# Causal mask of an attention's second pass: from mask matmuls to GpSimd selects, and the second pass first in each slot

## The chip, the cores and the metric

The kernel runs on one core of one Trainium2 chip. The metric is the device time of one execution in microseconds; the kernel before has a median of 624.34 us over three executions (624.0 to 624.88).

## The reference, cut to what matters

Two transformer layers on x of 4 sequences of 512 tokens with 128 channels (a state-space mixer and a mixture of experts, then attention and a second mixture of experts), each part behind an adaptive layer norm. The change touches the attention of the second layer alone: 16 heads of 8 channels, rotary positions, causal softmax.

```python
q = apply_rope(q); k = apply_rope(k)
scores = jnp.einsum('bhqd,bhkd->bhqk', q, k) / jnp.sqrt(dk)
causal = jnp.tril(jnp.ones((S, S), dtype=bool))
scores = jnp.where(causal, scores, -jnp.inf)
probs = jax.nn.softmax(scores, axis=-1)
attn = jnp.einsum('bhqk,bhkd->bhqd', probs, v)
return attn.transpose(0, 2, 1, 3).reshape(B, S, D) @ W_o.T
```

## The kernel before, in words

The five engines and SyncE each have their own program and meet at semaphores. What lies before attention and behind it is untouched by the change.

Attention works on 16 steps s = 4b + g: sequence b, group g of four heads. It has two passes. The **first pass** finds the maximum of each query's scores: `scores` (L1619) computes 16 score tiles of a step in 10 units on TensorE, each unit into one bank of a ring of three PSUM banks; VectorE's `maximum` (L1151) adds a mask that lies in SBUF and reduces each tile. Four small VectorE ops (`max_parts`, L1165 to L1172) split the negated maxima into three bf16 parts, `maxima_T` (L1629) transposes them, ScalarE evacuates them (L730), and SyncE writes them with four DMAs (L340) as three more rows of the augmented queries, the m rows. The keys have three rows of ones there (`k_ones`), so that a product of 51 rows gives the score less its maximum.

The **second pass** computes the transposed scores. `scores_T` (L1650) takes one key tile and one pair of heads, into two of the four PSUM banks 4 to 7; ahead of them four matmuls (L1645: two 64-column halves for each of two heads) write a causal mask of 0 and -1e30 into the 128 columns of the diagonal tile, and the scores are accumulated on top. ScalarE takes the exponential (`probs`, L701) of both heads into one of four buffers of pt. `weighted_values` (L1664) multiplies a pair of these by the values.

All engines follow one order, of rounds `it` from -2 to 16 and 8 slots i each: the first pass is of step it + 2, the second of step it. In slot i TensorE does the unit or units of `scores`, then `scores_T(8*it + i)`, which waits for the exponential of two slots before and, in slot 0, for the m rows, then in odd slots the weighted values of a pair of slots (in slot i those of i - 3 and i - 2), and the transposes and projections that have a place in this slot: `maxima_T` in 2, `o_T` (L1673) in 3, the projections of sequences 2 and 3 in rounds 2 and 6. ScalarE evacuates the finished output (L724) in slot 1, and VectorE divides it by its denominators in slot 3 (L1181, L1185), when `o_T` is there. In rounds 5, 9 and 13 VectorE also prepares the router's input (`router_input`, L367, L372, L386, L1123, L1128) in slots 2 to 6: in slot 4, L386 waits for GpSimd's `ln_rstd` (L379, L381).

GpSimd has little to do there: `rotate`, `rest` and `last_part` (L475, L481, L486) for the rotated queries and keys of each sequence, and `ln_rstd`, each as soon as its input is there. SyncE writes the parts of queries and keys to DRAM (12 DMAs, L312) and reads them back in the attention's layout (8 DMAs, L325); for sequences 2 and 3 it does so between the m rows of steps 4 and 5, and of 8 and 9.

Of the kernel before, what the change touches and what calls it, by code (L numbers as in the profile page):

```python
# [9 lines left out]
ALU = mybir.AluOpType  # L10
# [3 lines left out]
P = 128  # L14
B, S, D = 4, 512, 128
# [40 lines left out]
BPACK = [("identb", 128), ("causal", 256), ("half", 64), ("sel0", 1024)]  # L56
# [10 lines left out]
def adaln_kernel(nc, x_in, mod_in, mixw_in, moe0_in, attn_in, moe1_in, const_in, bconst_in, kones_in, out):  # L67
    with ExitStack() as ctx:
# [219 lines left out]
        def _(sp):  # L288
# [13 lines left out]
            for k in range(2):  # L302
                for hh in range(2):
                    sp.dma_start(kaug[HALF * hh + KR:HALF * hh + KM, k, :, :], kones_in).then_inc(sem("k_ones"), 16)
# [94 lines left out]
        def _(pool):  # L399
# [69 lines left out]

            def rotate(i):  # L470
# [27 lines left out]
            for b in range(1, B):  # L498
                if b == 3:
                    ln_rstd(pool, 4, 0)  # L500
                for stage in (rotate, rest, last_part):
                    stage(2 * b)
                    stage(2 * b + 1)
            for b in range(1, B):
                ln_rstd(pool, 4, b)
# [792 lines left out]
        def _(pe):  # L1298
# [308 lines left out]
            def scores(s, i):  # L1607
                b, g = divmod(s, QG)
                if g == 0 and i == 0:
                    pe.wait_ge(sem(f"aug_first{b % 2}"), 16 * 4 * (b // 2 + 1))  # L1610
                    pe.wait_ge(sem("k_ones"), 64)
# [21 lines left out]
            def scores_T(u):  # L1633
# [8 lines left out]
                for qh in range(2):  # L1642
                    for hh in range(2):
                        bank, lo = 4 + 2 * (u % 2) + hh, HALF * hh
                        pe.matmul(ps[:, bank, HALF * qh:HALF * (qh + 1)],  # L1645
                                  w["causal"][lo:lo + HALF, qh * P:(qh + 1) * P], w["half"][lo:lo + HALF, :],
                                  start=(qh == 0), stop=True, skip_group_check=True)
                for hh in range(2):
                    bank, lo = 4 + 2 * (u % 2) + hh, HALF * hh
                    mm = pe.matmul(ps[:, bank, 0:n], kaug[lo:lo + KM, b % 2, 2 * g + jp, kt * P:(kt + 1) * P],  # L1650
                                   qaug[lo:lo + KM, b % 2, 2 * g + jp, kt * P:S], start=False, stop=True,
                                   skip_group_check=True)
                mm.then_inc(sem("st_ps"), 1)

            def weighted_values(m):
# [5 lines left out]
                pe.wait_ge(sem("probs"), 2 * (m + 1))  # L1661
# [34 lines left out]
            for it in range(-2, 17):  # L1696
# [3 lines left out]
                for i in range(8):  # L1700
                    if it + 2 < 16:
                        for u in at_slot[i]:
                            scores(it + 2, u)
                    if 0 <= it < 16:
                        scores_T(8 * it + i)
# [59 lines left out]
def shape_constants():  # L1765
# [21 lines left out]
    for e in range(8):  # L1787
        for piece in range(3):
# [3 lines left out]
        "causal": np.concatenate([np.where(k[None, :] > k[:, None] % HALF + HALF * qh, NEG, 0.0) for qh in range(2)],  # L1792
                                 axis=1),
# [70 lines left out]
```

## Time and profile before

| | us |
|---|---|
| median of three executions | 624.34 |
| profiled execution | 620.97 |
| its span, first to last instruction | 619.2 |
| TensorE matmul, busy | 479.0 |
| VectorE, busy | 410.3 |
| ScalarE, busy | 278.0 |
| GpSimd, busy | 197.7 |
| mask matmuls (L1645), 512 of them, busy | 48.6 |
| attention, slot (0,0) to the last weighted values | 323.8 to 509.1 |

The busy times are from the page's first part. Matmuls overlap in the array and their ends are modelled, so that the times of TensorE's groups can't be added up; starts are better read than durations. The profiled execution lies 3.4 us below the median.

### The profile page before, as it was taken

The numbers are of one execution on the slowest core, as the hardware profiler recorded it, in microseconds if no ns is written. First come the engines' busy times: TensorE is split into PE (matmuls) and PEld (weight loads), VectorE is DVE, ScalarE is ACT, GpSimd is POOL, SyncE is SP. The second block draws the span as 40 slices with busy tenths as digits, with TensorE's granted clock in tenths as the row PEclk, the third lists the DMA queues.
The fourth block names the chain that finished last, engine by engine and source line by source line (L and its number), as shares of the span: only waits on it lengthen the run. The fifth ranks groups of instructions, "written<-read, shape, count | busy, mean of one in ns | idle before, by whom it ended". The sixth has DMA issues, their size and how long they took to land.

```text
span 619.2 us, 10103 instructions
## 1 busy us (share of the span) xinstructions
PE 479.0 (77%) x3167; PEld 283.4 (46%) x3167; DVE 410.3 (66%) x1363; ACT 278.0 (45%) x510; POOL 197.7 (32%) x254
## 2 busy tenths in 40 slices
PE   4697779886989999995589994998599786009990
PEld 4554567765634444442334442344245235009990
DVE  4788668996456767677787893788488804305543
ACT  2477876642235454532225681476357471002330
POOL 4300059995105544445500120031000000453443
PEclk9888899996599999999756996599779898558996
DMA  9500000001500000002860035006200000022014
GB/s 361 142 1 1 0 2 2 2 0 35 244 1 0 1 2 0 0 1 70 210 130 2 3 105 103 2 4 173 34 3 3 2 2 1 31 86 76 32 36 148
DMA packets 25083, 31.75 MB, mean 51 GB/s; under 512 B 2444, under 2 KB 22860, under 8 KB 24508
## 3 DMA queue, kind: packets, MB, share of 16 engines
q1 hardware_dynamic: 23784, 28.52, 16.4%
q0 software_dynamic: 1248, 2.59, 1.3%
q8 instruction: 27, 0.44, 0.3%
q14 instruction: 24, 0.20, 0.1%
HBM read 19.42 MB, written 11.48 MB: 50 GB/s over the span
## 4 chain that ended last, share of the span: by engine, by line
PE 52%; DVE 18%; issue 8%; ACT 7%; DMA 5%; POOL 5%; SPq 5%; DVEq 0%; ACTq 0%; POOLq 0%
PE ps L1664 5%; PE ps L1547 5%; PE ps L1551 4%; PE ps L1535 4%; DVE moe L1151 3%; PE ps L1748 3%; PE ps L1619 3%; PE ps L1570 3%; DVE rows L386 2%; POOL slots_x L512 2%; PE ps L1759 2%; PE ps L1650 2%; SPq L312 2%; PE ps L1352 2%; DMA arena<-arena 2%
## 5 line engine op out<-in xcount | busy, mean ns | idle before, releaser
L1151 DVE CUSTOM_DVE_ANT_0 moe<-ps,const 128x512 bf16<-128x512 f32 (+3 forms) x256 | 113.0, 487 | 25.9 <-PE ps L1619 24.8
L701 ACT ACTIVATE arena<-ps 128x256 f32<-128x256 f32 (+3 forms) x128 | 86.4, 702 | 66.6 <-PE ps L1650 65.7
L1619 PE MATMUL ps<-arena 48*128 48x128 bf16 (+3 forms) x256 | 61.1, 346 | 15.3 <-DVE arena L1151 13.9
L1645 PE MATMUL ps<-bconst 64*128 64x64 bf16 x512 | 48.6, 203 | 17.3 <-DMA arena<-arena 15.6
L461 POOL TENSOR_TENSOR arena<-arena 128x512 f32<-128x512 f32 x30 | 38.1, 1270 | 68.4 <-DVE arena L1053 68.2
L1650 PE MATMUL ps<-arena 51*128 51x128 bf16 (+3 forms) x256 | 57.0, 328 | 0.0
L1664 PE MATMUL ps<-arena 128*32 128x512 f32 (+3 forms) x512 | 55.2, 507 | 0.9 <-ACT arena L701 0.6
L379 POOL TENSOR_SCALAR rs<-mv 128x4 f32<-128x4 f32 x20 | 5.3, 264 | 139.7 <-DVE mv L372 139.2
L1619 PEld LDWEIGHTS ps<-arena 48*128 48x128 bf16 x256 | 17.2, 98 | 68.5 <-DVE arena L1151 42.8
L1645 PEld LDWEIGHTS ps<-bconst 64*128 64x128 bf16 x512 | 31.6, 102 | 32.1 <-DMA arena<-arena 17.5
L1044 DVE SCALAR_TENSOR_TENSOR arena<-ps,arena 128x512 f32<-128x512 f32 x32 | 22.1, 692 | 27.7 <-ACT arena L677 27.7
L749 ACT ACTIVATE arena<-ps 128x512 f32<-128x512 f32 x23 | 13.7, 597 | 54.6 <-PE ps L1748 35.2
L672 ACT ACTIVATE arena<-ps,moe 128x512 f32<-128x512 f32 x32 | 22.0, 687 | 34.5 <-PE ps L1547 34.5
L861 DVE SCALAR_TENSOR_TENSOR arena<-ps,mixw,arena 128x511 f32<-128x511 f32 (+2 forms) x48 | 33.2, 745 | 5.0 <-ACT arena L569 5.0
L1547 PE MATMUL ps<-arena,moe 128*128 128x512 f32 x64 | 32.9, 595 | 1.0 <-DVE arena L1038 1.0
L475 POOL TENSOR_TENSOR moe<-moe 128x512 f32<-128x512 f32 x8 | 10.2, 1270 | 72.4 <-DVE moe L1070 72.4
L1551 PE MATMUL ps<-arena,moe 128*128 128x512 f32 x64 | 32.7, 591 | 0.0
L1535 PE MATMUL ps<-arena,moe 128*128 128x512 f32 x64 | 32.5, 592 | 0.0
L518 POOL DMA_INDIRECT tokens_y<-arena,token_at x23 | 22.0, 957 | 32.1 <-DVE arena L1286 30.8
L1739 PE MATMUL ps<-const,arena 128*128 128x128 f32 x23 | 6.5, 293 | 29.3 <-DMA arena<-slots_x 29.3
L677 ACT ACTIVATE arena<-ps,moe 128x512 f32<-128x512 f32 x32 | 22.0, 687 | 13.0 <-PE ps L1551 13.0
L1748 PE MATMUL ps<-arena 128*128 128x128 f32 x184 | 26.1, 288 | 0.5 <-DVE arena L1282 0.3
(242 smaller groups left out, 1111.2 us busy)
## 6 DMA issues: line engine op xcount, KB each, us to landing
qk_parts<-arena SPq DMA_DIRECT2D x48, 128.0 KB, 2.3
arena<-qk_parts SPq DMA_DIRECT2D x16, 288.0 KB, 6.1
arena<-moe_in SPq DMA_DIRECT2D x1, 4100.0 KB, 14.0
moe<-moe_in SPq DMA_DIRECT2D x1, 1936.0 KB, 14.1
arena<-qk_parts SPq DMA_DIRECT2D x16, 96.0 KB, 2.2
slots_x<-zeros SPq DMA_DIRECT2D x1, 1518.0 KB, 20.5
arena<-slots_x SPq DMA_DIRECT2D x3, 396.0 KB, 4.3
const<-const_in SPq DMA_DIRECT2D x1, 1067.0 KB, 8.6
```

What stands on the lines that cost most here:

```text
L461: pool.tensor_tensor(yacc[:, ts], yacc[:, ts], pr[:, i % 2, :], ALU.add).then_inc(sem("yacc"), 1)
L701: act.activation(pt[:, u % 4, :, 0:n], ps[:, 4 + 2 * k:6 + 2 * k, 0:n], ACT.Exp, scale=ATT_SCALE).then_inc(sem("probs"), 1)
L861: v.scalar_tensor_tensor(out=acc[b % 2][:, c, s:S], in0=ps[:, c, 0:S - s], scalar=w["conv_w"][:, 4 * c + 3 - s:4 * c + 4 - s], in1=acc[b % ...
L1151: v.tensor_tensor_reduce(out=junk[:, done % 2, 0:n], in0=ps[:, k, col:col + n], in1=w["mask"][:, (3 - qt) * P:4 * P], scale=1.0, scalar=3 ...
L1535: pe.matmul(ps[:, 6 + i % 2, :], w["w2"][:, e * D:(e + 1) * D], gT[:, i % 2, :], start=True, stop=True).then_inc(sem("p2_ps"), 1)
L1547: pe.matmul(ps[:, 2 + i % 2, :], w["w1"][:, e * D:(e + 1) * D], xm[:, i % 2, :], start=True, stop=True).then_inc(sem("p1_ps"), 1)
L1551: pe.matmul(ps[:, 4 + i % 2, :], w["w3"][:, e * D:(e + 1) * D], xm[:, i % 2, :], start=True, stop=True).then_inc(sem("p3_ps"), 1)
L1619: mm = pe.matmul(ps[:, k, col:col + n], qaug[lo:lo + KR, b % 2, 2 * g + j // 2, qt * P:(qt + 1) * P], kaug[lo:lo + KR, b % 2, 2 * g + j // ...
L1645: pe.matmul(ps[:, bank, HALF * qh:HALF * (qh + 1)], w["causal"][lo:lo + HALF, qh * P:(qh + 1) * P], w["half"][lo:lo + HALF, :], start=(qh ...
L1650: mm = pe.matmul(ps[:, bank, 0:n], kaug[lo:lo + KM, b % 2, 2 * g + jp, kt * P:(kt + 1) * P], qaug[lo:lo + KM, b % 2, 2 * g + jp, kt * P:S] ...
L1664: mm = pe.matmul(ps[32 * j:32 * j + 32, 3, kt * P:S], va[:, b % 2, kt, 4 * (s % QG) + j, :], pt[:, (2 * m + j // 2) % 4, j % 2, 0:n], star ...
L1748: mm = pe.matmul(ps[:, j % 2, q * P:(q + 1) * P], w1[:, j % 2, q * P:(q + 1) * P], xT[:, j % 2, :], start=True, stop=True)
```

## The change

The four mask matmuls in front of `scores_T` are taken out, with their two constants; the scores no longer accumulate on a mask. In their place GpSimd runs one affine select on each slot's exponentials: in the 128 columns of the diagonal tile, for both heads, it keeps an element where the query is not before the key and writes 0 elsewhere. The weighted values wait for the selects (`masked`) and no more for the exponentials (`probs`). GpSimd's program becomes a loop over the same rounds and slots, in which `rotate`, `rest`, `last_part` and `ln_rstd` have fixed places behind the select of a slot. On TensorE `scores_T` moves ahead of `scores` in every slot. The semaphore `k_ones` is merged into `aug_first0`.

```diff
--- before.py
+++ after.py
@@ -53,7 +53,7 @@
     "const": [("ident", 128), ("tri", 128), ("after", 128), ("cos", 512), ("sin", 512), ("iota", 8),
               ("mask", 512), ("segment", NT * E1), ("full", NT), ("block", NBLK), ("number", NT), ("spare", NBLK)],
 }
-BPACK = [("identb", 128), ("causal", 256), ("half", 64), ("sel0", 1024)]
+BPACK = [("identb", 128), ("sel0", 1024)]
 
 
 def offsets(fields):
@@ -301,7 +301,8 @@
 
             for k in range(2):
                 for hh in range(2):
-                    sp.dma_start(kaug[HALF * hh + KR:HALF * hh + KM, k, :, :], kones_in).then_inc(sem("k_ones"), 16)
+                    sp.dma_start(kaug[HALF * hh + KR:HALF * hh + KM, k, :, :], kones_in)\
+                        .then_inc(sem("aug_first0"), 16)
 
             def parts_out(b, i):
 
@@ -467,6 +468,15 @@
                     pool.memset(va[:, :, :, :, DK:DK + 1], 1.0).then_inc(sem("va_clear"), 1)
 
 
+            nothing = pool.to_reg(0.0)
+
+            def causal(u):
+
+                pool.wait_ge(sem("probs"), u + 1)
+                own = pt[:, u % 4, :, 0:P]
+                pool.affine_select(own, own, pattern=[[0, 2], [1, P]], base=0, channel_multiplier=-1,
+                                   compare_op=ALU.is_ge, fill=nothing).then_inc(sem("masked"), 1)
+
             def rotate(i):
                 a = i % 2
                 pool.wait_ge(sem("rope"), 2 * (i + 1))
@@ -495,14 +505,26 @@
             last_part(1)
             ln_rstd(pool, 3, 2)
             ln_rstd(pool, 3, 3)
-            for b in range(1, B):
-                if b == 3:
-                    ln_rstd(pool, 4, 0)
-                for stage in (rotate, rest, last_part):
-                    stage(2 * b)
-                    stage(2 * b + 1)
-            for b in range(1, B):
-                ln_rstd(pool, 4, b)
+            for stage in (rotate, rest, last_part):
+                stage(2)
+                stage(3)
+            for it in range(17):
+                for i in range(8):
+                    if it < 16:
+                        causal(8 * it + i)
+                    if it in (2, 6):
+                        b = (it + 6) // 4
+                        if i in (3, 7):
+                            rotate(2 * b + i // 4)
+                    if it in (3, 7):
+                        b = (it + 5) // 4
+                        if i in (2, 3):
+                            rest(2 * b + i - 2)
+                        elif i in (5, 6):
+                            last_part(2 * b + i - 5)
+                    if it in (5, 9, 13) and i == 5:
+                        ln_rstd(pool, 4, it // 4 - 1)
+            ln_rstd(pool, 4, B - 1)
 
             pool.wait_ge(sem("posu"), 1)
             pool.wait_ge(sem("numbers"), 2)
@@ -1607,8 +1629,7 @@
             def scores(s, i):
                 b, g = divmod(s, QG)
                 if g == 0 and i == 0:
-                    pe.wait_ge(sem(f"aug_first{b % 2}"), 16 * 4 * (b // 2 + 1))
-                    pe.wait_ge(sem("k_ones"), 64)
+                    pe.wait_ge(sem(f"aug_first{b % 2}"), 64 * (b // 2 + 2 - b % 2))
                 elif g == 1 and i == 0:
                     pe.wait_ge(sem(f"aug{b % 2}"), 16 * 4 * (b // 2 + 1))
                 k = ring_bank("mx", s, i)
@@ -1639,17 +1660,10 @@
                     pe.wait_ge(sem(f"m_rows{s % 2}"), 64 * (s // 2 + 1))
                 if u >= 2:
                     pe.wait_ge(sem("probs"), u - 1)
-                for qh in range(2):
-                    for hh in range(2):
-                        bank, lo = 4 + 2 * (u % 2) + hh, HALF * hh
-                        pe.matmul(ps[:, bank, HALF * qh:HALF * (qh + 1)],
-                                  w["causal"][lo:lo + HALF, qh * P:(qh + 1) * P], w["half"][lo:lo + HALF, :],
-                                  start=(qh == 0), stop=True, skip_group_check=True)
                 for hh in range(2):
                     bank, lo = 4 + 2 * (u % 2) + hh, HALF * hh
                     mm = pe.matmul(ps[:, bank, 0:n], kaug[lo:lo + KM, b % 2, 2 * g + jp, kt * P:(kt + 1) * P],
-                                   qaug[lo:lo + KM, b % 2, 2 * g + jp, kt * P:S], start=False, stop=True,
-                                   skip_group_check=True)
+                                   qaug[lo:lo + KM, b % 2, 2 * g + jp, kt * P:S], start=True, stop=True)
                 mm.then_inc(sem("st_ps"), 1)
 
             def weighted_values(m):
@@ -1658,7 +1672,7 @@
                 n = S - kt * P
                 if i == 0 and s >= 1:
                     pe.wait_ge(sem("ot"), s)
-                pe.wait_ge(sem("probs"), 2 * (m + 1))
+                pe.wait_ge(sem("masked"), 2 * (m + 1))
                 pe.wait_ge(sem("va"), b + 1)
                 for j in range(4):
                     mm = pe.matmul(ps[32 * j:32 * j + 32, 3, kt * P:S], va[:, b % 2, kt, 4 * (s % QG) + j, :],
@@ -1698,11 +1712,11 @@
                     transposes(3, 2, bank=4)
                     transposes(3, 3, bank=4)
                 for i in range(8):
+                    if 0 <= it < 16:
+                        scores_T(8 * it + i)
                     if it + 2 < 16:
                         for u in at_slot[i]:
                             scores(it + 2, u)
-                    if 0 <= it < 16:
-                        scores_T(8 * it + i)
                     if i % 2 == 1 and 0 <= 4 * it + i // 2 - 1 < 64:
                         weighted_values(4 * it + i // 2 - 1)
                     if i == 2 and 0 <= it + 1 < 16:
@@ -1789,9 +1803,6 @@
             sel0[8 * piece + e, e, :] = 1.0
     bconst = {
         "identb": np.eye(P),
-        "causal": np.concatenate([np.where(k[None, :] > k[:, None] % HALF + HALF * qh, NEG, 0.0) for qh in range(2)],
-                                 axis=1),
-        "half": k[:, None] % HALF == np.arange(HALF)[None, :],
         "sel0": sel0.reshape(P, -1),
     }
     fc = np.concatenate([np.asarray(const[n], np.float32) for n, _ in PACKS["const"]], axis=1)
```

## Rows read from the trace of the kernel before

**Rows 1.** rounds 0, 1, 2, 11: length, busy PE PEld DVE ACT POOL, clock, DMA, GB/s

```profile
323.82:334.86 11.04, 10.05 (x94) 4.47 (x96) 8.27 (x41) 6.11 (x9) 0.00 (x0) 0.50 0.00 1
334.86:343.16 8.30, 8.05 (x107) 3.95 (x107) 7.30 (x34) 5.92 (x10) 0.00 (x0) 0.94 0.01 4
343.16:355.28 12.12, 12.12 (x116) 5.03 (x118) 10.52 (x43) 6.58 (x11) 1.99 (x2) 1.00 0.01 3
...
461.31:469.73 8.42, 7.80 (x108) 3.76 (x109) 7.85 (x39) 6.36 (x11) 0.00 (x0) 1.00 0.01 3
```

**Rows 2.** timeline of round 11: start us, us, engine line op form xcount [idle before]

```profile
461.79 0.66 ACT L701 ACTIVATE arena<-ps 128x256 f32<-128x256 f32 x2 [0.20 <-PE ps L1650]
...
462.61 0.17 DVE L1167 SCALAR_TENSOR_TENSOR arena<-arena 128x16 f32<-128x16 f32 x1
...
465.65 0.26 DVE L1181 RECIPROCAL arena<-ps 128x16 f32<-128x16 f32 x1 [0.34 <-PE ps L1673]
```

**Rows 3.** the page, granted clock in 40 slices of 15.5 us, in tenths

```profile
PEclk9888899996599999999756996599779898558996
```

**Rows 4.** chain of waits, 358 to 384 us: start us, us, what

```profile
358.45 0.58 ACT arena L730
...
368.50 0.60 SPq L312
...
377.53 5.54 DMA arena<-arena
...
383.12 0.29 PE ps L1645 x4
```

**Rows 5.** waits of TensorE in attention: us in total, times, longest

```profile
PE ps L1645 <- DMA arena<-arena: 15.6, 2, 8.3
```

**Rows 6.** timeline of TensorE, full clock at 355.6, half clock at 383.7

```profile
355.60 0.23 PE L1645 MATMUL ps<-bconst 64*128 64x64 bf16 x4
...
355.67 0.22 PE L1650 MATMUL ps<-arena 51*128 51x128 bf16 x2
...
383.74 0.31 PE L1645 MATMUL ps<-bconst 64*128 64x64 bf16 x2
...
383.87 0.29 PE L1650 MATMUL ps<-arena 51*128 51x128 bf16 x1
```

**Rows 7.** timeline of round 13, slots 4 to 7

```profile
485.34 1.51 ACT L701 ACTIVATE arena<-ps 128x768 f32<-128x768 f32 x2 [0.90 <-PE ps L1650]
...
485.88 0.23 POOL L379 TENSOR_SCALAR rs<-mv 128x4 f32<-128x4 f32 x1 [39.76 <-DVE mv L372]
...
487.26 1.12 DVE L386 TENSOR_SCALAR rows<-x,mv,rs 128x128 f32<-128x128 f32 x4 [0.81 <-POOL rs L381]
...
490.33 0.50 PE L1619 MATMUL ps<-arena 48*128 48x384 bf16 x1 [0.82 <-DVE arena L1151]
...
490.85 0.61 PE L1650 MATMUL ps<-arena 51*128 51x512 bf16 x1
```

**Rows 8.** GpSimd's groups by line and form: busy us, mean ns

```profile
L423 POOL TENSOR_TENSOR arena<-arena,mixw 128x256 f32<-128x256 f32 x16 | 11.7, 729 | 0.0
...
L459 POOL COPY arena<-arena 128x512 f32<-128x512 f32 x2 | 1.2, 608 | 3.0 <-DVE arena L1053 3.0
```

**Rows 9.** timeline of the end of attention

```profile
508.04 1.07 PE L1664 MATMUL ps<-arena 128*32 128x512 f32 x8 [0.60 <-ACT arena L701]
```

**Rows 10.** line L386 alone: duration ns min/median/max, first and last start

```profile
L386 DVE TENSOR_SCALAR rows<-x,mv,rs x48: 315/344/1189, 121.2 to 518.7; 128x128 f32<-128x128 f32 x48
```

**Rows 11.** timeline of VectorE beside GpSimd, at 303 and at 355 us

```profile
303.08 5.31 DVE L386 TENSOR_SCALAR rows<-x,mv,rs 128x128 f32<-128x128 f32 x6
...
303.58 2.26 POOL L481 TENSOR_TENSOR moe<-moe,arena 128x512 f32<-128x512 f32 x2
...
354.56 1.28 POOL L475 TENSOR_TENSOR moe<-moe 128x512 f32<-128x512 f32 x1 [4.53 <-DVE moe L1070]
...
355.10 0.56 DVE L1151 CUSTOM_DVE_ANT_0 moe<-ps,const 128x384 bf16<-128x384 f32 x1
```

## The prediction

> **What bounds the kernel now.** I read the page first: of 619.2 us, attention with its two interleaved passes is the stretch from slot (0,0) at 323.8 us to the last weighted values at 509.1 us, and all that the diff touches lies in it. (I write (it,i) for slot i of round it.) Then the windows, one for each round [rows 1]: at full clock a plain round takes 8.3 to 8.4 us, of which VectorE is busy 7.3 to 7.9; round 11 leaves it 8.42 - 7.85 = 0.57 us idle, 0.34 of it in front of the reciprocal, which waits for o_T [rows 2]. TensorE also looks full there (7.80), but its ends are modelled. In rounds 2 and 6, where it has the projections too, it is the later one (12.12 of 12.12). At half clock (round 0, 0.50) it is the bound as well: 10.05 of 11.04. The page's clock row [rows 3] and the windows put about 30 of the 128 slots at half clock.
>
> The chain of waits shows something that no engine's speed changes [rows 4]: from the evacuation of mT(4) in (3,2) at 358.45 SyncE issues 4 + 12 + 8 + 4 DMAs one behind the other, and (5,0) starts when the last has landed, at 383.12. TensorE waits 8.3 us there, and nearly as long again in (9,0): 15.6 us in two waits [rows 5]. What is won between (3,2) and (5,0) or (7,2) and (9,0), 28 slots in all, makes these waits longer and ends nothing earlier. 100 slots are left in which time can be won or lost.
>
> **The change part by part.** The sum is made against the profiled execution (620.97 us around a span of 619.2), which is 3.4 us below the median of 624.34; the difference is added to the median.
>
> *512 mask matmuls go.* A slot loses two 64-column matmuls in each row group, and the groups run side by side: from the first mask matmul to the scores behind it are 355.67 - 355.60 = 0.07 us at full clock, 383.87 - 383.74 = 0.13 at half [rows 6]. The page's 48.6 us of busy time for the line is pipeline depth counted over and over. Outside the two fixed stretches I count 23 half-clock slots with TensorE last (rounds 0, 5, 9, 10 and 13/14 in part): 3.0 us; and 27 at full clock (rounds 2, 6, 14, 15): 1.9. In the others VectorE is last and the edit is worth nothing. The half clock ends in the trace at moments of its own and not after so much work, so I take a quarter off the first: **-4.1 us**. Bounds: 0, and 23 x 0.13 + 77 x 0.07 = -8.4.
>
> *The second pass goes first in each slot.* ScalarE gets its scores before TensorE stands at a ring bank that VectorE still reads. Of VectorE's idle 0.57 us a plain round can give back half (bounds 0 and all): five rounds, -1.2. In rounds 5, 9 and 13 the scores of slot 7 wait at 490.33 and both second-pass matmuls (to 490.85) come behind them [rows 7]; now they are done before: 0.5 each, -1.5. Sum **-2.7**. Against it: in (5,0) and (9,0) the first-pass matmul used to be issued before the wait for the m rows and now stands behind it: 0.4 us of work at half clock each, **+0.8** (bounds 0 and 1.2).
>
> *128 selects on GpSimd.* The trace has none. From below, the one-input COPY of 128x512 at 608 ns makes about 0.36 us for 256 elements; from above, the two-input op on 512 elements, 1.27. The nearest row is the two-input op on 256 elements, 0.73 [rows 8]; with one input less I take 0.6, and 0.15 for two semaphores. 128 x 0.6 = 77 us lie beside other work: the pair that the weighted values need was exponentiated two slots before. It shows where ScalarE is last: behind the 1.02 us exponential of slot 7 in (it,1). In rounds with a first pass, the exponentials start some 0.3 us earlier by the new order and pay for it; in (15,1) I take 0.5, and behind the very last exponential all 0.75, since the weighted values at 508.04 already wait for it [rows 9]: **+1.25** (bounds 0.5 and 2.8). In the Trainium skill, GPSIMD Engine Reference, section 7 gives compare-and-select bodies 1.03 to 2.03 cycles an element; an estimate from that page is 0.2 to 0.45 us for 256, and the sum would be about 3 us lower; no run here shows it yet.
>
> *ln_rstd of rounds 5, 9, 13 moves behind a select.* GpSimd is strictly in order. Today it starts when the moments are there and VectorE's L386 in slot 4 waits for it until 487.26; variance and power take it from 485.88, 1.4 us [rows 7]. Now it stands behind causal(8it+5), that is behind the exponential of slot 5, which ends at 485.34 + 1.51 = 486.85, perhaps 0.25 earlier by the new order. 486.6 + 0.07 + 0.6 + 1.4 = 488.7: 1.4 us later. Behind L386 are queued the maxima of slots 5 to 7, which free the ring for TensorE. Three rounds: **+4.2** (bounds 0, if the delay is covered, and 6).
>
> *GpSimd is now busy beside VectorE.* L386 takes 344 ns in the median, and up to 1189 ns; the long ones lie in 303.08 to 308.39, 5.31 us for six of them under GpSimd's back-to-back ops of 1.1 to 1.3 us [rows 10, 11]. So some VectorE ops wait for a whole GpSimd op. The maxima (L1151) don't: 0.56 us under a GpSimd op like elsewhere [rows 11]. Exposed are the router's ops in rounds 5, 9, 13 (four L386, two products and sums, the residual sum) and the four small ops that split the maxima in slots 0 and 1 (L1165 to L1172). The exponentials of slots 7, 0 and 1 come close together (two in 1.0 us from 461.79, [rows 2]), so four selects stand back to back on GpSimd just where L1167 runs (462.61) and, before it, L1165; these ops never met GpSimd in the trace. Bounds for a round: 0 and 4 x 0.6 = 2.4; I take 0.7, two of them caught for a little over half a select. VectorE is last in some 7 rounds outside the fixed stretches: **+4.9**. The router's ops: 0.8 in each of three rounds (bounds 0 and 2), **+2.4**. In the Trainium skill, SBUF — State Buffer, section "Who interferes with whom" has this as an exclusive port pair: a VectorE op in a two-port mode or with two SBUF inputs against a GpSimd op that reads SBUF, while an op with one SBUF input goes free. The trace agrees: 1189 ns for L386, and no effect on L1151, which reads PSUM and one SBUF tile.
>
> *Rotate, rest, last_part between selects, k_ones on aug_first0, a narrower bconst.* In rounds 2/3 and 6/7 GpSimd gets 16 selects of 0.6 and the six old ops of some 1.2: 16.8 us of work in some 21: the last part is there about 1 us before SyncE issues its last DMA of the parts at 368.50 [rows 4]. Cover: SyncE's own issues. 0; if a select takes 0.9, 3 us late.
>
> Sum: -4.1 - 2.7 + 0.8 + 1.25 + 4.2 + 4.9 + 2.4 = **+6.75**; 624.34 + 6.75 = **631.1 us**.
>
> **The rivals.**
> - *TensorE's order paces every round* (for: 7.80 of 8.42 us busy in round 11; against: VectorE's 7.85 [rows 1]). All 100 slots pay: -8.4, the order -2.7, +0.8, +1.25, half of the ln_rstd term since VectorE has room, +2.1: -7.0, **617.3**. It decides if VectorE's small ops don't wait for GpSimd and a select stays below 0.4 us. Chance 0.13.
> - *A short select and no port waits on the small ops* (for: COPY at 608 ns; against: L386's 1189 ns). The terms of 4.9 and 2.4 go, 1.0 less for the shorter select: -1.5, **622.8**, up to 624.5 with a few waits. Chance 0.17, 0.10 of it within 0.2%.
> - *A long select, 0.9 us or more* (for: 0.73 to 0.81 us for 256 elements with two inputs). Port terms half as much again (+3.7), ln_rstd +0.9, tail +0.6, and the parts of rounds 3 and 7 late by 10 x 0.3 less the 1 us of room, twice (+4): **640**; from 1.04 us on GpSimd would pace every slot. Chance 0.14.
> - *The clock comes back one step later* after the waits in rounds 5 and 9, with less for TensorE to do: 6.8 us at 11.04 instead of 8.30 a round is 1.7 us, twice: **634.5**. Chance 0.09.
>
> **How the numbers follow.** My forecast has 0.47, between 627 and 635. Faster by over 0.2% (1.25 us, about what a measurement of this kernel can tell from no change): 0.13 + 0.07 = 0.20. Within it: 0.10 + 0.02 = 0.12. Slower: 0.68. The range takes in most of the first rival and the long select: 619.5 to 642.
>
> **What would show it.** The select's mean on GpSimd (0.6). Plain rounds at full clock: 8.4 us before, 8.8 to 9.2 after, with L1165, L1167, L1170 and L1172 above 0.2 us. L386 in rounds 5, 9, 13 starting about 1.4 us later behind the moments, and longer. The waits of some 8 us at (5,0) and (9,0) still there, each a little longer where the stretch before has become faster. The last weighted values 0.75 us behind the last exponential. I am wrong if the small ops keep their 0.18 us and plain rounds fall below 8.2.

## The result: 1% slower, by a sum whose terms were partly wrong

Changed kernel: 631.22 us in the median of 4 runs, against 624.61 us for the kernel before on the same chip, ratio 1.0132 (95% interval 1.0087 to 1.0176). Two later comparisons on other chips gave 1.0085 (1.005 to 1.0121) and 1.0103 (1.0064 to 1.0141). Weighted by their intervals the three make **1.0103 ± 0.0023**, that is 6.4 us of 623. The predicted ratio was 631.1 / 624.34 = 1.0108. Executions more than 1.5% longer than the fastest of their kernel are left out of the ratios; in the second comparison these were three of twelve, and with them its medians are 629.43 and 623.17 us, a ratio of 1.0100.

The edit moves the line numbers. In the changed kernel L477 is the select, L723 the exponential, L1173 the maximum of the first pass (L1151 before), L1640 the first pass's scores (L1619), L1665 the second pass's (L1650), L1650 `maxima_T` (L1629), L752 the evacuation of its result (L730), L1678 the weighted values (L1664), L380 and L382 the two operations of ln_rstd (L379, L381), L387 the router's normalisation (L386), and L1187, L1189, L1192 and L1194 the four small operations that split the maxima (L1165 to L1172).

The windows of the changed kernel answer to [rows 1] (columns as there: stretch and length, busy time of PE, PEld, DVE, ACT and POOL with the number of instructions, granted clock, DMA share, GB/s): rounds 0, 1, 2, 11, and then 13 and 15.

```profile
323.28:333.89 10.61, 9.44 (x61) 2.95 (x62) 8.26 (x40) 5.88 (x9) 3.26 (x8) 0.50 0.01 2
333.89:344.71 10.82, 10.46 (x76) 3.63 (x73) 7.53 (x33) 6.41 (x10) 2.91 (x8) 0.63 0.01 3
344.71:356.52 11.81, 11.78 (x84) 3.93 (x81) 10.54 (x43) 6.57 (x10) 4.42 (x9) 1.00 0.01 2
...
463.72:472.10 8.38, 7.26 (x76) 2.85 (x72) 7.87 (x39) 6.15 (x10) 3.20 (x9) 1.00 0.01 3
...
482.05:496.36 14.31, 8.70 (x75) 2.83 (x74) 12.20 (x51) 6.17 (x10) 4.82 (x10) 0.85 0.00 1
...
504.05:512.74 8.69, 6.58 (x60) 1.82 (x60) 0.55 (x2) 5.70 (x10) 3.61 (x9) 1.00 0.00 0
```

Round 0, at half clock under TensorE, fell from 11.04 to 10.61 us, and round 2 from 12.12 to 11.81. The plain round 11 did not grow to the 8.8 to 9.2 us that I had given as the mark of my theory: 8.42 became 8.38. Round 1 grew by 2.5 us because the full clock came back 6 us later in this execution (0.63 instead of 0.94); it came back as late in two of the three profiles of this kernel, and in one of a kernel beside it, so I take nothing from it. Round 13 went from 13.24 to 14.31, and round 15 to the end of attention from 8.29 to 8.69.

The select is shorter than I took, and VectorE waits longer for ln_rstd. First the page's group of the select, then the waits of VectorE in attention (engine, line, waited for: us in total, times, longest), which were 2.4 us in three before:

```profile
L477 POOL TENSOR_SCALAR_AFFINE_SELECT arena<-arena 128x256 f32<-128x256 f32 x128 | 51.9, 410 | 134.6 <-ACT arena L723 133.5
```

```profile
DVE rows L387 <- POOL rs L382: 5.9, 3, 2.2
```

The chain of waits in round 5 (start us, us, what) shows the path that I had priced: exponential of slot 5, select, variance and power of ln_rstd, then the four normalisations on VectorE, with the maxima behind them.

```profile
392.77 0.82 ACT arena L723
393.59 0.06 issue
393.65 0.41 POOL arena L477
394.06 0.21 POOL rs L380
394.27 0.07 issue
394.34 1.05 POOL rs L382
...
395.76 0.93 DVE rows L387 x3
396.69 0.33 DVE moe L1173
```

TensorE's waits for the DMAs in attention stand nearly as [rows 5] had them, 16.3 us in four against 15.6 in two; the one in front of (5,0) lasts 8.4. Its waits for the maxima of the first pass, which free the ring, were 7.9 us in 11 before, and are 12.3 in 10 now:

```profile
PE ps L1665 <- DMA arena<-arena: 16.3, 4, 8.4
PE ps L1640 <- DVE arena L1173: 12.3, 10, 3.3
PE ps L1650 <- DVE arena L1194: 7.4, 6, 1.7
PE ps L1678 <- POOL arena L477: 2.5, 4, 1.0
```

### The profile page after: what moved, and what is told of

Its sections match the earlier page's. It is cut to its first block, busy times and chain, and to the rows that moved or that the text cites. A ratio compares the mean times of both kernels' runs of the same rounds, so it can differ in the third digit from the quotient of the medians.

```text
span 624.8 us, 9208 instructions
## 1 busy us (share of the span) xinstructions
PE 473.6 (76%) x2655; PEld 268.4 (43%) x2655; DVE 415.2 (66%) x1363; ACT 277.3 (44%) x510; POOL 248.7 (40%) x382
## 4 chain that ended last, share of the span: by engine, by line
PE 52%; DVE 18%; issue 9%; ACT 6%; DMA 6%; POOL 5%; SPq 5%; DVEq 0%; POOLq 0%; ACTq 0%
PE ps L1678 5%; PE ps L1569 4%; PE ps L1573 4%; PE ps L1557 4%; DVE moe L1173 3%; PE ps L1762 3%; PE ps L1640 3%; PE ps L1773 2%; DVE rows L387 2%; PE ps L1665 2%; POOL slots_x L534 2%; PE ps L1592 2%; PE ps L1374 2%; SPq L313 2%; DMA arena<-arena 2%
## 5 line engine op out<-in xcount | busy, mean ns | idle before, releaser
L1173 DVE CUSTOM_DVE_ANT_0 moe<-ps,const 128x512 bf16<-128x512 f32 (+3 forms) x256 | 113.0, 486 | 25.3 <-PE ps L1640 24.9
L723 ACT ACTIVATE arena<-ps 128x256 f32<-128x256 f32 (+3 forms) x128 | 85.5, 700 | 63.4 <-PE ps L1665 62.6
L477 POOL TENSOR_SCALAR_AFFINE_SELECT arena<-arena 128x256 f32<-128x256 f32 x128 | 51.9, 410 | 134.6 <-ACT arena L723 133.5
L1640 PE MATMUL ps<-arena 48*128 48x128 bf16 (+3 forms) x256 | 59.3, 351 | 19.5 <-DVE arena L1173 18.3
L1665 PE MATMUL ps<-arena 51*128 51x128 bf16 (+3 forms) x256 | 44.6, 332 | 18.7 <-DMA arena<-arena 16.3
L1678 PE MATMUL ps<-arena 128*32 128x512 f32 (+3 forms) x512 | 56.3, 517 | 3.2 <-POOL arena L477 2.5
L1665 PEld LDWEIGHTS ps<-arena 51*128 51x128 bf16 x256 | 12.9, 97 | 70.1 <-ACT arena L723 25.7
L1640 PEld LDWEIGHTS ps<-arena 48*128 48x128 bf16 x256 | 21.7, 103 | 37.1 <-DVE arena L1173 30.5
L422 POOL TENSOR_TENSOR arena<-arena 128x256 f32<-128x256 f32 x16 | 12.4, 773 | 44.2 <-DVE arena L866 40.5
L1350 PE MATMUL ps<-const,rows 128*128 128x128 f32 x64 | 14.9, 393 | 13.9 <-DVE rows L387 10.4
```

What stands on the lines that cost most here:

```text
L477: pool.affine_select(own, own, pattern=[[0, 2], [1, P]], base=0, channel_multiplier=-1, compare_op=ALU.is_ge, fill=nothing).then_inc(sem(" ...
L723: act.activation(pt[:, u % 4, :, 0:n], ps[:, 4 + 2 * k:6 + 2 * k, 0:n], ACT.Exp, scale=ATT_SCALE).then_inc(sem("probs"), 1)
L1173: v.tensor_tensor_reduce(out=junk[:, done % 2, 0:n], in0=ps[:, k, col:col + n], in1=w["mask"][:, (3 - qt) * P:4 * P], scale=1.0, scalar=3 ...
L1640: mm = pe.matmul(ps[:, k, col:col + n], qaug[lo:lo + KR, b % 2, 2 * g + j // 2, qt * P:(qt + 1) * P], kaug[lo:lo + KR, b % 2, 2 * g + j // ...
L1678: mm = pe.matmul(ps[32 * j:32 * j + 32, 3, kt * P:S], va[:, b % 2, kt, 4 * (s % QG) + j, :], pt[:, (2 * m + j // 2) % 4, j % 2, 0:n], star ...
```

## The experiments

Each was timed beside the kernel before, and the ratios are against it.

### Which part costs: four kernels on one chip

**ln_rstd at slot 3 of its round instead of slot 5**

```diff
-                    if it in (5, 9, 13) and i == 5:
+                    if it in (5, 9, 13) and i == 3:
                         ln_rstd(pool, 4, it // 4 - 1)
```

> The changed kernel, with ln_rstd of rounds 5, 9 and 13 placed behind the select of slot 3 instead of slot 5. Theory (ln_rstd queued behind selects holds VectorE): the wait of L387 for it falls from 5.9 us in three times to about 3, and the kernel gains 2.5 to 3.5 us: 628. Rival (latency of the selects before the weighted values is what costs): no more than 1 us, 630 to 631. Rival (the clock): times scatter as before, with no link to this edit.

Measured: 1.0042 (1.0012 to 1.0072); VectorE's waits for it fell from 5.9 to 2.1 us, and TensorE's waits for the maxima that are queued behind them from 12.3 to 7.7. At first sight that is more than half of the loss, but the changed kernel was not on this chip, so the pair was repeated below.

**The mask matmuls kept as dummies in the changed kernel** (they write the bank that the scores then overwrite)

```diff
+                for qh in range(2):
+                    for hh in range(2):
+                        pe.matmul(ps[:, bank, HALF * qh:HALF * (qh + 1)], w["causal"]..., w["half"]..., start=True, stop=True)
                 for hh in range(2):
```

> The changed kernel, with the four mask matmuls of each slot still issued, into the banks that the scores then overwrite: TensorE has the same to do as before, and nothing else changes. Rival (the clock: with less to do TensorE is granted its full clock later): the mean granted clock goes back to 0.857 and the time falls, to 626 to 628. Theory (mask matmuls cost 0.07 us a slot at full and 0.13 at half clock where TensorE is last): it rises by 2 to 4 us, to 633 to 635, whatever the clock does.

Measured: 1.0116 (1.0068 to 1.0163), against 1.0103 for the changed kernel. 512 matmuls more cost 0.8 ± 3.3 us, which these intervals can't tell from nothing; my price of 4.1 us for taking them out is at the very edge. The granted clock rose as the rival said (0.856 in the mean), but the time did not fall.

**The order alone, in the kernel before**

```diff
                 for i in range(8):
+                    if 0 <= it < 16:
+                        scores_T(8 * it + i)
                     if it + 2 < 16:
                         for u in at_slot[i]:
                             scores(it + 2, u)
-                    if 0 <= it < 16:
-                        scores_T(8 * it + i)
```

> The kernel before, with the second pass ahead of the first in each slot and nothing else (mask matmuls and GpSimd as before). Theory: the exponentials come earlier and the scores of slot 7 in rounds 5, 9, 13 are done before the ring frees: 621.5 to 623 against 624.6. Rival (first-pass scores come later and VectorE, which is last, starves): 625.5 to 627.

Measured: 0.9985 (0.9956 to 1.0013), -0.9 ± 1.8 us: the rival, 1.0014 or more, is just outside the interval, and most of the theory's 0.9950 to 0.9974 is inside, as is no effect at all. Its round 11 is no shorter (8.56 us against 8.42, first row below).

**The changed kernel without its selects** (the causal mask of the second pass is left out; GpSimd's old operations in their old order, the weighted values wait for `probs`)

```diff
-                    if it < 16:
-                        causal(8 * it + i)
...
-                pe.wait_ge(sem("masked"), 2 * (m + 1))
+                pe.wait_ge(sem("probs"), 2 * (m + 1))
```

> The changed kernel with the selects left out and no mask in their place (the second pass is computed without its causal mask), GpSimd's other work placed as before. Theory: masks gone and new order without what the selects cost, 6.8 us under 624.6: 618. Bound by VectorE alone it would be 621. Rival (the clock): with the mask matmuls gone the granted clock is 0.83 to 0.84 here too and the time stays at 622 to 626.

Measured: 0.9967 (0.994 to 0.9995). Order and masks together are worth -2.1 ± 1.7 us, not the -6.0 of my sum. On the scale of 624.6 it is 622.5 us, where the clock's rival had it (622 to 626), though the granted clock of 0.854 did not fall to that rival's 0.83 to 0.84. Everything that GpSimd brings costs 1.0103 - 0.9967 = 0.0136, 8.5 ± 2.2 us. Round 11 with the order alone, then without masks and selects, then, from an experiment below, with two selects in each slot:

```profile
457.86:466.42 8.56, 7.66 (x109) 3.37 (x110) 7.99 (x40) 6.27 (x10) 0.00 (x0) 1.00 0.01 3
```

```profile
460.98:469.34 8.36, 7.27 (x76) 2.85 (x73) 7.85 (x39) 6.15 (x10) 0.00 (x0) 1.00 0.01 3
```

```profile
460.06:468.58 8.52, 7.35 (x77) 2.86 (x74) 8.01 (x39) 6.15 (x10) 6.03 (x17) 1.00 0.01 3
```

GpSimd's 0, 3.20 and 6.03 busy us leave a plain round at 8.36, 8.38 and 8.52 us.

### Load or latency: four kernels on a second chip

**The changed kernel again**, with no edit

> The changed kernel unchanged, to have it on one chip with the runs beside it. Theory (the change costs by two mechanisms of about the same size, ln_rstd behind the select of slot 5 and VectorE's operations beside the selects, less some 0.3% for order and masks): ratio 1.012 to 1.014, as in the first comparison (1.0132), and 0.009 above the kernel with ln_rstd at slot 3 (1.0042). Rival (the first comparison was of another chip, and ln_rstd's place is worth only VectorE's 3.5 us of waits that can be read, 0.006): ratio 1.009 to 1.011. VectorE waits 5.5 to 6.2 us for L382 in both.

Measured: 1.0085 (1.005 to 1.0121); lower than the first and than my 1.012 to 1.014, nearest to the rival's 1.009 to 1.011, and the intervals overlap.

**Selects on an unused tile** (ln_rstd at slot 3; causal mask of the second pass left out; each select also waits for the fourth one before it)

```diff
-                own = pt[:, u % 4, :, 0:P]
+                own = packed["mixw"]...[:, u % 4]
...
-                pe.wait_ge(sem("masked"), 2 * (m + 1))
+                pe.wait_ge(sem("probs"), 2 * (m + 1))
```

> Kernel with ln_rstd at slot 3, but the selects run on an unused tile of the same shape (the causal mask of the second pass is left out) and the weighted values wait for the exponentials only. GpSimd does the same work at the same times beside VectorE; no latency is on the path. The kernel without selects was 0.9967, the one with ln_rstd at slot 3 1.0042: 4.7 us between them. Theory (the cost is VectorE's operations held up by GpSimd): 1.003 to 1.004, small operations of VectorE at their means of the changed kernel (L1187 0.36, L1189 0.24 us). Rival (the cost is the select's latency between exponential and weighted values, in the tail and behind slot 7): 0.997 to 0.999, with the small operations just as long. Expected by the first: 1.0035.

Measured: 1.0006 (0.9977 to 1.0034), between the two theories. Of the 0.0070 between the kernel without selects and the one with ln_rstd early, 0.0039 is load beside VectorE and 0.0031 the wait for the select, each ± 0.004: so both may be there, and by the times their split is not settled. The traces settle part of it, as the section on the terms shows.

**Two selects in each slot** (ln_rstd at slot 3)

```diff
+                pool.affine_select(spare, spare, ...).then_inc(sem("spare_masked"), 1)
                 own = pt[:, u % 4, :, 0:P]
```

> Kernel with ln_rstd at slot 3, with a second select on an unused tile ahead of the real one in every slot: GpSimd is busy 0.82 us instead of 0.41 in a slot, and the weighted values get their exponentials 0.4 us later. Theory (VectorE held up): the small operations meet a select nearly always, another 0.3 us in each of some 7 rounds, and the router's operations too, with 0.4 us in the tail and 0.4 in (15,1): +3 us, ratio 1.009 to 1.010. Rival (latency decides): 0.4 us behind slot 7 in every round with VectorE or ScalarE last, +5 us or more: 1.012 to 1.014. If neither matters and the 4.7 us were something else (the order of GpSimd's old work): 1.004 to 1.006.

Measured: 1.0054 (1.0027 to 1.0082), 0.0017 ± 0.0034 or 1.1 ± 2.1 us above one select. Of what I had written down, the third case holds, 1.004 to 1.006 if neither mechanism matters much; the 3 us of my theory are at the edge of the difference and its ratio of 1.009 to 1.010 is outside the interval, and the rival's 5 us are out. But this kernel also shows where a second select hides. TensorE's waits for selects rose from 2.5 us in 4 to 8.4 in 14, and from slot 2 to slot 2 rounds 3 and 7 take 11.97 and 11.82 us (clock 0.70 and 0.88) where one select has 9.29 and 10.01 (1.00 and 0.83). These rounds lie in front of the waits for the DMAs, which shrank from 14.8 to 5.8 us; a kernel without that cover would pay more.

**First pass first again, in the changed kernel** (the two calls back in their old order, nothing else)

> The changed kernel with the first pass's matmuls ahead of the second's in every slot, as before. Theory (order was worth -2.7 + 0.8 us in the sum; the kernel before with the order alone gave 0.9985): 0.0015 to 0.003 above the changed kernel on the same chip, 1.015 to 1.016. Rival (with selects behind the exponentials the earlier scores of the second pass matter more, since they pay for the select): 1.018 or more, with the waits of TensorE for L477 above 2.5 us. Second rival (the order is worth nothing or costs): 1.013 or less.

Measured: 1.0116 (1.0075 to 1.0156), inconclusive against 1.0103 ± 0.0023; it lies where the second rival had it, at 1.013 or less, and the first rival's 1.018 is out. TensorE's waits for the select rose from 2.5 us in 4 to 3.9 us in 8, and VectorE's for ln_rstd from 5.9 to 7.5, which is the direction of the first rival, and too little for it.

### The two places in GpSimd's order: four kernels on a third chip

**The changed kernel, the base**, with no edit

> The changed kernel again, as the common base for the three runs beside it (so far 1.0132 and 1.0085 on two chips). Expected 1.010 to 1.011. It serves the comparison alone.

Measured: 1.0103 (1.0064 to 1.0141).

**ln_rstd at slot 3, repeated**

> The changed kernel with ln_rstd ahead of the selects of slots 4 and 5 instead of behind them, now on one chip with the changed kernel. Theory (ln_rstd's place costs what VectorE is seen to wait, 5.9 against 2.1 us in three waits): 3 to 4 us, 0.005 to 0.006 below the changed kernel, so 1.005. Rival (it costs nothing: the two earlier ratios were of two chips, and VectorE's waits in rounds 5 and 9 lie under the clock's phases): within 0.002 of the changed kernel.

Measured: 1.0032 (1.0005 to 1.006), 0.0071 ± 0.0047 or 4.4 ± 2.9 us below the base. With the earlier runs, 1.0103 ± 0.0023 less 1.0037 ± 0.0020 is 0.0066 ± 0.0031: **4.1 ± 1.9 us**, where I had +4.2. Round 13 of the two kernels shows it at nearly the same clock (0.62 and 0.65). Timeline of the base, round 13 (start us, us, engine, line, operation, form, count, idle before):

```profile
491.61 1.56 ACT L723 ACTIVATE arena<-ps 128x768 f32<-128x768 f32 x2 [1.76 <-PE ps L1665]
...
493.24 0.41 POOL L477 TENSOR_SCALAR_AFFINE_SELECT arena<-arena 128x256 f32<-128x256 f32 x1 [0.34 <-ACT arena L723]
...
493.61 0.23 POOL L380 TENSOR_SCALAR rs<-mv 128x4 f32<-128x4 f32 x1
...
495.00 1.40 DVE L387 TENSOR_SCALAR rows<-x,mv,rs 128x128 f32<-128x128 f32 x4 [2.19 <-POOL rs L382]
```

The same with ln_rstd at slot 3:

```profile
487.78 1.56 ACT L723 ACTIVATE arena<-ps 128x768 f32<-128x768 f32 x2 [1.72 <-PE ps L1665]
...
488.30 0.23 POOL L380 TENSOR_SCALAR rs<-mv 128x4 f32<-128x4 f32 x1 [1.76 <-DVE mv L373]
...
489.69 1.30 DVE L387 TENSOR_SCALAR rows<-x,mv,rs 128x128 f32<-128x128 f32 x4 [0.71 <-POOL rs L382]
```

From the exponential to L387 it is 495.00 - 491.61 = 3.39 us in the one and 489.69 - 487.78 = 1.91 in the other: 1.48 us of delay, where the prediction had 1.4. Windows of rounds 5, 9 and 13, of the base and then with ln_rstd early:

```profile
385.11:399.41 14.30, 10.39 (x73) 3.16 (x74) 10.79 (x48) 6.26 (x10) 4.42 (x10) 0.74 0.00 1
441.54:457.08 15.54, 12.04 (x72) 3.69 (x73) 11.08 (x48) 6.41 (x10) 4.51 (x10) 0.61 0.01 2
484.50:500.33 15.83, 11.08 (x74) 3.53 (x74) 12.58 (x51) 6.30 (x10) 4.89 (x10) 0.62 0.00 1
```

```profile
384.61:398.56 13.95, 11.56 (x74) 3.61 (x74) 10.99 (x48) 6.41 (x10) 4.84 (x10) 0.62 0.00 1
439.25:453.22 13.97, 11.54 (x72) 3.62 (x73) 10.99 (x48) 6.41 (x10) 4.90 (x10) 0.62 0.01 3
480.91:494.92 14.01, 10.83 (x75) 3.41 (x74) 12.40 (x51) 6.31 (x10) 4.93 (x10) 0.65 0.00 1
```

45.67 against 41.93 us: 3.7 us lie in just these rounds. The two spans differ by more, 630.4 against 621.8; 3.1 us of the rest come after the end of attention (113.2 and 110.1 us), where the clock's phases differ.

**ln_rstd at slot 3, and the second rotate of rounds 2 and 6 at slot 6 instead of 7**

```diff
-                        if i in (3, 7):
+                        if i in (3, 6):
                             rotate(2 * b + i // 4)
```

> ln_rstd at slot 3 and the second rotate of rounds 2 and 6 at slot 6 instead of 7. Theory: in the changed kernel L1187 of rounds 3 and 7 lasts 0.83 us because it stands under the 1.27 us addition of the rotate, which the select of slot 7 pushed back from 354.56 to 356.90; mT(4) is evacuated 3.84 us after the start of round 3 instead of 3.17, and the fixed stretch starts that much later, twice. With the rotate a slot earlier L1187 meets at most a select: 0.4 to 0.6 us, evacuation 3.4 to 3.5 us after the start, 0.8 us less in all; ratio 1.003 to 1.004. Rival (the select of (2,7), now behind the rotate and 0.7 us later, holds the weighted values and with them TensorE): round 3 as long as before, evacuation at 3.8 or later, ratio 1.005 or more.

Measured: 1.0031 (1.0008 to 1.0053), the same as the 1.0032 beside it. In the trace the rival's mechanism holds; its ratio of 1.005 or more did not come, and the 0.0013 that the theory wanted is less than these runs can tell. The timeline of the changed kernel at the start of round 3 has what I wanted to remove, L1187 held for 0.83 us until the addition of the rotate (L485) ends at 358.17, and mT(4)'s evacuation 360.36 - 356.52 = 3.84 us after the start of the round, where it was 358.45 - 355.28 = 3.17:

```profile
356.52 0.23 PE L1665 MATMUL ps<-arena 51*128 51x128 bf16 x2
...
356.90 1.27 POOL L485 TENSOR_TENSOR moe<-moe 128x512 f32<-128x512 f32 x1
...
357.39 0.83 DVE L1187 TENSOR_SCALAR arena<-arena 128x16 bf16<-128x16 f32 x1
...
360.36 0.59 ACT L752 ACTIVATE arena<-ps 12x512 bf16<-12x512 bf16 x1 [0.61 <-PE ps L1650]
```

With the rotate a slot earlier (round 3 starts at 355.34):

```profile
354.87 1.27 POOL L485 TENSOR_TENSOR moe<-moe 128x512 f32<-128x512 f32 x1 [0.71 <-DVE moe L1092]
...
356.09 1.13 POOL L477 TENSOR_SCALAR_AFFINE_SELECT arena<-arena 128x256 f32<-128x256 f32 x3
356.21 0.33 DVE L1187 TENSOR_SCALAR arena<-arena 128x16 bf16<-128x16 f32 x1
...
356.55 0.16 PEld L1678 LDWEIGHTS ps<-arena 128*32 128x32 f32 x8 [0.94 <-POOL arena L477]
...
359.18 0.57 ACT L752 ACTIVATE arena<-ps 12x512 bf16<-12x512 bf16 x1
```

L1187 gets its half microsecond back, the select of (2,7) is now the one that comes late, TensorE waits 0.94 us for it, and the evacuation starts 359.18 - 355.34 = 3.84 us after the start as before. The same stands in round 7, 415.21 - 411.37 = 3.84. The wait changed its owner.

**As before it, and round 15 masked by matmuls again** (nothing of the computation is left out)

```diff
-                    if it < 16:
+                    if it < 15:
                         causal(8 * it + i)
...
-                pe.wait_ge(sem("masked"), 2 * (m + 1))
+                pe.wait_ge(sem("masked" if m < 60 else "probs"), 2 * (m + 1))
```

> As the kernel with both moved early, and in round 15 the causal mask by matmuls again, so that the weighted values there wait for the exponentials alone. The computation is complete. Theory (tail of 0.4 us idle and select of 0.41, less the masks of eight slots): attention ends 0.5 to 0.9 us earlier after the start of round 15 (8.69 becomes 7.9 to 8.3 us, 8.30 in the kernel before), ratio 0.001 lower, 1.002. Rival (the half clock at the end of attention decides, masks or not): no difference to the kernel beside it.

Measured: 1.0011 (0.9982 to 1.004). Round 15 with selects, then with masks:

```profile
501.96:510.98 9.02, 6.63 (x60) 1.83 (x60) 0.55 (x2) 6.03 (x10) 3.58 (x10) 1.00 0.00 0
```

```profile
500.72:509.21 8.49, 6.91 (x92) 2.31 (x92) 0.55 (x2) 5.95 (x10) 0.41 (x1) 1.00 0.01 2
```

0.53 us shorter, the lower end of the 0.5 to 0.9 that I expected, though 8.49 us misses the 7.9 to 8.3 that I had written beside it. The time fell by 0.0020 ± 0.0037, which is not clear of nothing. This is the fastest kernel with selects, and not faster than the kernel before; nor is the order alone, within its interval.

## Why the prediction came out right, term by term

The time is right by luck in two of its three parts: two wrong terms of about 4 us stand against each other. The third, ln_rstd, which I priced from one place of one trace, is right by itself, in mechanism and size. Of the five marks that I gave, two came as written (L387 1.48 us later, the waits of 8 us still there); the select's 0.6 us, plain rounds of 8.8 to 9.2 and the 0.75 us of the tail did not.

| term | predicted | measured | from |
|---|---|---|---|
| masks gone, order, first pass behind the m rows | -4.1 - 2.7 + 0.8 = -6.0 | -2.1 ± 1.7 | no selects |
| ln_rstd behind the select of slot 5 | +4.2 | +4.1 ± 1.9 | ln_rstd at slot 3, twice |
| select exposed, small operations, router's | 1.25 + 4.9 + 2.4 = +8.55 | +4.4 ± 2.1 | ln_rstd early less no selects |
| sum | +6.75 | +6.4 | |

**Masks gone: mis-sized at half clock.** What each edit does at full clock can be read without the scatter of the clock, in stretches from one evacuation of `maxima_T`'s result (slot 2) to the next, for five rounds in which the granted clock is 1.00 in every kernel named (us, differences of two starts of that evacuation):

| stretch from slot 2 of round | before | order alone | no masks, no selects | changed kernel | with dummies |
|---|---|---|---|---|---|
| 1 | 9.27 | 9.34 | 8.79 | 8.83 | 9.35 |
| 2 | 11.33 | 11.33 | 11.05 | 11.74 | 12.03 |
| 6 | 11.33 | 11.32 | 11.01 | 11.62 | 12.18 |
| 11 | 8.43 | 8.57 | 8.37 | 8.38 | 8.65 |
| 12 | 10.71 | 10.71 | 10.40 | 10.76 | 11.12 |

(The 8.83 is of the changed kernel's third comparison, since in the other two the clock was lower there; its other rows are of the first.) From the second column to the third, taking the masks out gave 0.55, 0.28, 0.31, 0.20 and 0.31 us, 1.65 in all; from the fifth to the fourth 0.52, 0.29, 0.56, 0.27 and 0.36, 2.0 in all. So the 1.9 that I had for full clock is about right, though it came in plain rounds too, where I had nothing. What did not show in the times is the rest of the term, 3.0 us at half clock less a quarter; round 0, wholly at half clock, did become 0.43 us shorter, of the 8 x 0.13 = 1.0 that I had. Two pairs point to where it went. With the dummies the timed runs had a mean granted clock of 0.856, without them 0.843 (0.855 to 0.857 in the kernel before), at a time that can't be told apart; and from the order alone (0.862) to no masks and no selects (0.854) the time fell by 0.0018 ± 0.0040, 1.1 us, only. The windows over the whole of attention say the same, changed kernel in its second comparison, then with dummies:

```profile
323.24:516.82 193.58, 153.12 (x1180) 55.16 (x1180) 138.50 (x600) 105.22 (x169) 69.20 (x146) 0.81 0.15 35
```

```profile
322.66:513.05 190.39, 151.95 (x1690) 64.31 (x1692) 137.90 (x606) 105.90 (x169) 69.35 (x146) 0.87 0.15 36
```

TensorE issued 510 matmuls fewer and was at 1.2 GHz for more of the stretch. As 2 x (1 - clock) is the share at the lower level, an estimate from these two rows is 74 us of it without the dummies and 50 with them; the other two profiles of the changed kernel have 0.84 and 0.82 there, the kernel before 0.85. The step of the prediction that they speak against is "The half clock ends in the trace at moments of its own and not after so much work, so I take a quarter off the first": a quarter was far too little. That less work makes the half clock last longer is what the pairs agree on; it is not proved by them, since the clock's steps fall differently in every execution, and the cause stays open.

**The order: nothing in plain rounds.** I let VectorE's 0.57 us of idle time give back half, in five rounds (which is 1.4 us; the 1.2 in the sum is a slip). With the order alone it kept it: 8.56 - 7.99 = 0.57, and the table's plain stretch is 0.14 us longer than before. The idle time "in front of the reciprocal, which waits for o_T" was no slack that earlier scores could use.

**Small operations: the other failed step.** "I take 0.7, two of them caught for a little over half a select" was wrong in size and in who holds them. Their excess is 0.28 us a round in the mean of the 16, 4.5 us in all, and 2.4 of that is not owed to selects: L1187 took 828, 729, 824 and 720 ns in rounds 3, 4, 7 and 8, each time under one of GpSimd's old operations of some 1.2 us (L485 of `rotate`, L496 of `last_part`), which the selects had pushed into its way. Where a select was running at its start it took 269 to 380 ns, and in a plain round the excess hid in VectorE's idle time:

```profile
464.44 0.77 POOL L477 TENSOR_SCALAR_AFFINE_SELECT arena<-arena 128x256 f32<-128x256 f32 x2 [0.36 <-ACT arena L723]
464.60 0.28 DVE L1187 TENSOR_SCALAR arena<-arena 128x16 bf16<-128x16 f32 x1
...
465.40 0.17 DVE L1189 SCALAR_TENSOR_TENSOR arena<-arena 128x16 f32<-128x16 f32 x1
465.60 0.18 DVE L1192 CAST arena<-arena 128x16 bf16<-128x16 f32 x1
466.33 0.18 DVE L1194 TENSOR_TENSOR arena<-arena 128x16 bf16<-128x16 f32 x1
```

What counts of it is the 0.67 us at the head of rounds 3 and 7, 1.3 us in all, because the fixed stretch begins at that evacuation. The table has the same as 11.74 - 11.05 = 0.69 and 11.62 - 11.01 = 0.61 us, and the kernel with its selects on an unused tile, where no weighted values wait for them, takes 11.73 and 11.61 there: in these rounds the cost is GpSimd's load beside VectorE and not the wait for the select. The 0.36 us of the last stretch are the head of round 13, where the residual addition (L1217) took 842 ns instead of 691 and L1187 380 instead of 182. That makes 1.7 us that the traces show, where the two terms on VectorE's operations had 7.3; what is left of the measured +4.4 ± 2.1 beyond these and the tail is not located. The prediction had looked at rotate and its companions only for SyncE's transfers ("0"), not for whom they meet on VectorE.

**The router's operations** were hardly touched: the twelve L387 took 382 ns in the mean against 344, 0.15 us a round instead of the 0.8 that I gave to all of them.

**The tail** is right in kind: the last weighted values start 0.98 us after TensorE is free, against 0.60 [rows 9], and 511.68 - 510.10 - 1.04 = 0.54 us behind the end of the last exponential, where it was 0.05 before and I had added 0.75.

```profile
510.10 1.04 ACT L723 ACTIVATE arena<-ps 128x1024 f32<-128x1024 f32 x1
...
511.21 0.41 POOL L477 TENSOR_SCALAR_AFFINE_SELECT arena<-arena 128x256 f32<-128x256 f32 x1 [0.51 <-ACT arena L723]
...
511.68 1.06 PE L1678 MATMUL ps<-arena 128*32 128x512 f32 x8 [0.98 <-POOL arena L477]
```

**The select's length.** 410 ns, not 600. I took the nearest row, an operation with two inputs; below 0.41 lay the COPY's 0.36. The Trainium skill's range (GPSIMD Engine Reference, section 7), from which I had estimated 0.2 to 0.45 us, holds it.

**Left open.** After the end of attention the changed kernel takes 112.0 us against 110.0, at a clock of 0.74 against 0.77, although nothing there was changed. The other two profiles of it have 111.2 and 113.2, the two with ln_rstd early 112.1 and 110.1. Part of the loss may lie in the phase at which attention hands over to the clock; no run here separates it.

## What to carry to other kernels

Work put on an in-order engine costs by what it stands in front of. Here 52 us of selects, with the old operations that they displaced, cost 4.4 ± 2.1 us, a second 52 us about 1 more (with part of it hidden behind waits for DMAs), and one 1.3 us job of ln_rstd placed behind the select of slot 5 instead of slot 3 cost 4.1 ± 1.9 us in three rounds: before adding waits to such a queue, list who waits for each job already in it, and place those ahead of the new wait. Take work saved on a busy engine at half clock as unearned until a run shows it.

## What the runs showed of the hardware

- An affine select of 128x256 f32 takes 406 ns on GpSimd in the median of 128 (mean 410, 401 to 857), 0.77 us for two back to back.
- Which of two operations starts first decides who pays. L1187 took 183 ns at 324.01, where a select started 0.06 us after it, and 269 to 380 ns where one was already running; under a 1.27 us addition it lasted until 0.04 us after its end. The other way round, the select that started at 483.1, some 0.2 us behind VectorE's residual addition (L1217), took 857 ns. In the Trainium skill, SBUF — State Buffer, "Who interferes with whom" has it that whoever issues first holds the shared pair for the whole instruction; it says so of VectorE's two-port modes, and no run here shows which mode L1187 is in, but the trace agrees (828 ns behind the addition against 183 ahead of a select).
- The maxima, which read PSUM, took 276 to 693 ns over all 256 in the changed kernel, selects and additions beside them or not, and 283 to 693 before. L1194 never started under a GpSimd operation there and kept its 182 ns.
